# Attention results kept undivided, their softmax sums inverted apart and applied to turned results in the gating stage

## What is computed

```python
def _attention(src, Wq, bq, Wk, bk, Wv, bv, Wo, bo):
    q = (src @ Wq + bq).reshape(B, T, NHEAD, HEAD_DIM)   # k and v alike
    scores = jnp.einsum('bqhd,bkhd->bhqk', q, k) * scale
    probs = jax.nn.softmax(scores, axis=-1)
    out = jnp.einsum('bhqk,bkhd->bqhd', probs, v).reshape(B, T, d)
    return out @ Wo + bo
...
attn_out = _attention(src, Wq, bq, Wk, bk, Wv, bv, Wo, bo)
x = _ln(src + attn_out, ln1_g, ln1_b)
ff = _moe(x, gW, gb, W1, b1, W2, b2)      # softmax gates over 8 experts, two taken
return _ln(x + ff, ln2_g, ln2_b)
```

## Time and profile before

| | us |
|---|---|
| runs (3), median | 3671.24 (3670.13 to 3675.24) |
| the profiled execution | 3671.02 |
| its span, first to last instruction | 3669.3 |
| PE busy in the span | 3233.4 (88%) |
| DVE busy | 2949.0 (80%) |
| ScalarE busy | 2058.9 (56%) |
| POOL busy | 1198.9 (33%) |
| DVE's maxima L999, 2048 of them | 1285.6 |
| value products L1084 | 657.4 |
| first-pass products L1055 | 584.0 |

### The profile page before, as it was taken

How to read it: one execution, slowest core, us unless ns; L and a number is a source line. 1 busy time by engine, 2 the same in 40 slices (tenths; PEclk the granted TensorE clock), 3 DMA queues, 4 the chain that set the end, 5 groups by cost and what they waited for, 6 DMA issues and landing times. The chain is left out here.

```text
span 3669.3 us, 87949 instructions
## 1 busy us (share of the span) xinstructions
PE 3233.4 (88%) x34874; PEld 1861.1 (51%) x34875; DVE 2949.0 (80%) x4783; ACT 2058.9 (56%) x2972; POOL 1198.9 (33%) x974
## 2 busy tenths in 40 slices
PE   4889999999999999985999776996899999967776
PEld 1543333333333333344666542343787787756665
DVE  5778999999999999926666454775799999948986
ACT  0317777777777777763011265665675756434553
POOL 0310000000000000006011560000899999927875
PEclk8869999999999999996999877998999999989998
DMA  1552012020202020027222363333543434231110
GB/s 58 189 156 26 20 31 45 5 45 5 46 10 56 22 56 6 5 69 274 62 66 65 90 206 110 135 111 135 151 125 114 143 107 132 70 123 50 57 35 18
DMA packets 223122, 296.00 MB, mean 81 GB/s; under 512 B 72873, under 2 KB 159537, under 8 KB 220593
## 3 DMA queue, kind: packets, MB, share of 16 engines
q1 hardware_dynamic: 211616, 264.14, 25.3%
q0 software_dynamic: 6144, 17.05, 1.4%
q10 hardware_dynamic: 5008, 9.80, 0.7%
HBM read 174.35 MB, written 115.95 MB: 79 GB/s over the span
## 5 line engine op out<-in xcount | busy, mean ns | idle before, releaser
L999 DVE TENSOR_REDUCE att_maxima<-att_ps_m 128x1 f32<-128x512 f32 x2048 | 1285.6, 684 | 63.9 <-PE att_ps_m L1055 62.3
L954 ACT ACTIVATE att_probs<-att_ps_s 128x1024 f32<-128x1024 f32 x1024 | 999.4, 1022 | 280.3 <-PE att_ps_o L1084 267.8
L1084 PE MATMUL att_ps_o<-att_probs,held_vs 128*32 128x256 f32 x8192 | 657.4, 393 | 4.8 <-ACT att_probs L954 0.6
L2440 POOL TENSOR_TENSOR ss_ch<-ss_h,ss_c_rep 128x1024 f32<-128x1024 f32 x256 | 601.2, 2385 | 9.1 <-DVE ss_h L2527 9.1
L1055 PE MATMUL att_ps_m<-held_ks,held_qs 48*128 48x512 f32 x2048 | 584.0, 511 | 14.0 <-PEq L60 13.3
L2559 PE MATMUL ss_ps_u<-ss_diag,ss_dx_t 128*32 128x128 f32 x16384 | 475.3, 274 | 30.9 <-DMA ss_dx_t<-scratch_dx_t 15.0
L2559 PEld LDWEIGHTS ss_ps_u<-ss_diag,ss_dx_t 128*32 128x32 f32 x16384 | 455.5, 111 | 85.0 <-issue 68.7
L1055 PEld LDWEIGHTS att_ps_m<-held_ks,held_qs 48*128 48x128 f32 x2048 | 238.0, 188 | 456.8 <-DVE att_maxima L999 389.9
L1070 PE MATMUL att_ps_s<-held_qs,held_ks 50*128 50x512 f32 x2048 | 454.0, 405 | 2.8 <-ACT att_probs L954 0.8
L2479 ACT ACTIVATE ss_decay<-ss_delta,ss_a_neg 128x1024 f32<-128x1024 f32 x256 | 293.8, 1148 | 228.5 <-DVE ss_h L2527 206.8
L1084 PEld LDWEIGHTS att_ps_o<-att_probs,held_vs 128*32 128x32 f32 x8192 | 162.6, 108 | 361.6 <-issue 340.4
(11 more groups left out here) (394 smaller groups left out, 4485.2 us busy)
## 6 DMA issues: line engine op xcount, KB each, us to landing
ss_delta<-scratch_delta SPq DMA_DIRECT2D x256, 128.0 KB, 3.1
held_qs<-scratch_q SPq DMA_DIRECT2D x96, 128.0 KB, 4.6
held_ks<-scratch_k SPq DMA_DIRECT2D x96, 128.0 KB, 5.0
ex_x<-scratch_sorted_x SPq DMA_DIRECT2D x72, 132.0 KB, 2.1
scratch_sorted_y<-ex_y SPq DMA_DIRECT2D x72, 128.0 KB, 1.7
scratch_q<-held_parts SPq DMA_DIRECT2D x16, 512.0 KB, 4.7
scratch_k<-held_parts SPq DMA_DIRECT2D x16, 512.0 KB, 5.5
moe_w_w<-in_W SPq DMA_DIRECT2D x16, 512.0 KB
```

Source lines behind the costliest of these rows:

```text
L954: act.activation(probs[:, (2 * n + pair) % 4, :, :], ps_s[pair][:, :, :], ACT.Exp, scale=HD ** -0.5).then_inc(exp_done, 1)
L999: dve.tensor_reduce(maxima[:, j, at:at + 1], ps_m[plan.bank(key)][:, :], AX.X, ALU.max).then_inc(maxed, 1)
L1084: mm = pe.matmul(ps_o[h * VW:(h + 1) * VW, cols], vs[st // QC % 2][:, kt, h * VW:(h + 1) * VW], probs[:, (2 * n + h // 2) % 4, h % 2, cols ...
L2440: pool.tensor_tensor(ch[:, w.n % (CH_GROUPS * DQ), :], h[:, w.n % H_SLOTS, :], c_rep[:, w.ng, :], ALU.mult).then_inc(s["ch_ready"], 1)
```

## The change

The sums are no longer applied in attention. ScalarE's copy of `ps_o` has two slots now, and SP stores its rows of results as they are, by channel, to `scratch.outs`: four DMAs, one a head. Row 16 of each head, the sums of 512 queries, is spread by a DMA over 32 partitions of 16 columns, four DMAs a step. DVE inverts the 128x16 sums in key tile 10 (INVERT) and splits each inverse in a high part of the type fp32r and the rest; both go to `scratch.inv` by four DMAs. PE's transposes, ScalarE's second copy and POOL's division are gone, and the banks of `ps_m` are dealt out without `out`. All 16 columns after a head's values are ones.

In gating the results arrive turned, so `heads_t` is loaded directly, in two slots. The inverses of 16 heads in two parts (32 partitions) are spread over the 256 channels by two products with a pattern `own_head` of ones where a channel belongs to a head (`spread`), one step ahead of the rest, and DVE multiplies (`divide`, last in its step). PE's transposes of heads and ScalarE's copy are gone. POOL makes the pattern at the start, and SP copies it twice.

```diff
-                    pool.memset(by_head[:, :, HD:HD + 1], 1.0).then_inc(v_set, 1)
-                    pool.memset(by_head[:, :, HD + 1:VW], 0.0).then_inc(v_set, 1)
+                    pool.memset(by_head[:, :, HD:VW], 1.0).then_inc(v_set, 1)
...
-                if st > 0 and kt == 1:
-                    order.append(("out", st - 1))
...
+INVERT = 10
...
+                def store_outs(st):
+                    head, cols = places_of(st)
+                    sp.wait_ge(o_copied, st + 1)
+                    for h in range(QH):
+                        sp.dma_start(scratch.outs[(head + h) * HD:(head + h + 1) * HD, cols], o_sb[h * VW:h * VW + HD, st % 2, :]).then_inc(outs_stored[st % 2], 16)
+                    if st > 0:
+                        sp.wait_ge(sums_inverted, st)
+                    for h in range(QH):
+                        sp.dma_start(sums[h * VW:(h + 1) * VW, :], o_sb[h * VW + HD:h * VW + HD + 1, st % 2, :]).then_inc(sums_spread, 16)
+                def store_inv(st):
+                    head, cols = places_of(st)
+                    sp.wait_ge(inv_split, st + 1)
+                    for h in range(QH):
+                        sp.dma_start(scratch.inv[:, head + h, cols].rearrange("a (p j) -> p a j", p=VW),
+                                     inv_parts[h * VW:(h + 1) * VW, :, :].bitcast(F32)).then_inc(inv_stored, 16)
...
                 for st in range(1, STEPS):
+                    store_outs(st - 1)
                     if st % QC == 0 and st // QC + 1 < NQ:
...
-                    store_heads(st - 1)
                     if st + 1 < STEPS:
                         store_shift(st + 1)
+                    store_inv(st - 1)
...
-                        if st > 0 and kt == 4:
-                            divide(st - 1)
...
-                    act.activation(o_sb[:, :], ps_o[:, :], ACT.Copy).then_inc(o_copied, 1)
-                def copy_turned(st):
...
+                    if st >= 2:
+                        act.wait_ge(outs_stored[st % 2], st // 2 * QH * 16)
+                        act.wait_ge(sums_spread, (st - 1) * QH * 16)
+                    act.activation(o_sb[:, st % 2, :], ps_o[:, :], ACT.Copy).then_inc(o_copied, 1)
...
-                    dve.wait_ge(o_t_ready, st + 1)
+                    dve.wait_ge(sums_spread, (st + 1) * QH * 16)
                     if st > 0:
-                        dve.wait_ge(heads_ready, st)
-                    dve.reciprocal(sums[:, :], o_t[:, :, HD]).then_inc(sums_ready, 1)
+                        dve.wait_ge(inv_stored, st * QH * 16)
+                    dve.reciprocal(inv[:, :], sums[:, :]).then_inc(sums_inverted, 1)
+                    dve.wait_ge(sums_inverted, st + 1)
+                    split_high(dve, inv_parts[:, 0, :], inv[:, :]).then_inc(inv_high, 1)
+                    dve.wait_ge(inv_high, st + 1)
+                    split_low(dve, inv_parts[:, 1, :], inv[:, :], inv_parts[:, 0, :]).then_inc(inv_split, 1)
...
-                        if st > 0 and kt == 3:
+                        if st > 0 and kt == INVERT:
                             invert_sums(st - 1)
...
-                        if st > 0 and kt == 1:
-                            turn_out(st - 1)
...
                 load_heads(0, 0)
+                load_inv(0, 0)
+                load_inv(1, 1)
+                sp.wait_ge(own_set, 3)
+                for half in range(HALVES_QK):
+                    sp.dma_start(own_head[half * HEADS:(half + 1) * HEADS, :, :].bitcast(F32), own[:, :, :]).then_inc(own_copied, 16)
                 sp.dma_start(wo[:, :, :], io["Wo"].rearrange("(k p) c -> p k c", p=P)).then_inc(wo_loaded, 16)
...
+                def divide(g, slot):
+                    dve.wait_ge(heads_loaded[slot], (g // 2 + 1) * 16)
+                    dve.wait_ge(inv_spread, g + 1)
+                    dve.tensor_tensor(heads_t[:, slot, :, :], heads_t[:, slot, :, :], ps_h[:, :, :], ALU.mult).then_inc(heads_t_ready, 1)
...
-                run_stages(dve, GROUPS, (add_src, 1), (find_places, 4), (shift_logits, 3), (find_scale, 1), (take_best, 3), unroll=True)
+                run_stages(dve, GROUPS, (add_src, 1), (find_places, 4), (shift_logits, 3), (find_scale, 1), (take_best, 3), (divide, -1), unroll=True)
...
-                            mm = pe.transpose(ps_h[:, k, t * P:(t + 1) * P], heads[:, slot, t, k * P:(k + 1) * P], ident[:, :])
-                    mm.then_inc(heads_turned, 1)
+                    for k in range(KC):
+                        mm = pe.matmul(ps_h[:, k, :], own_head[:, k, :], inv[:, slot, :], start=True, stop=True)
+                    mm.then_inc(inv_spread, 1)
...
-                run_stages(pe, GROUPS, (turn_heads, 0), (count, 4), (turn_rows, 2), (product, 0), (logits, 2), unroll=True)
+                run_stages(pe, GROUPS, (spread, -1), (count, 4), (turn_rows, 2), (product, 0), (logits, 2), unroll=True)
```

94 lines of the change are left out of this document (43 added, 51 removed).

## The result

The changed kernel took 3681.14 us in the median of 20 executions (3669.94 to 3691.49), the kernel before 3672.53 us beside it (20 executions, 3664.55 to 3686.03): a ratio of 1.0021, 95% interval 1.0014 to 1.0029. The forecast was 3673.8 us with a range of 3664 to 3681 and a sum of +2.7 us on the kernel before; the ratio says +7.7 us (+5.1 to +10.7), just over the bound of 0.2%. So the change costs some 5 us more than forecast, and the result leans to "slower" where "no change" was thought likeliest.

The account below looks back on a forecast made before the run. PE and DVE, with no slack to speak of, bound attention; POOL's scatters bound gating. Attention -4.9, hand-over +6.1 and gating +1.5 make +2.7 on 3671.0 (0.2 under the median): 3673.8 us, range 3664 to 3681.

Parts of the forecast that it names:

- (a): Attention step: four transposes of the result leave PE, which both PE and DVE lose; -0.59 us a step.
- (b): Attention step: the old inversion in the fourth key tile, 0.24 us on DVE, goes; counted as -0.05 us a step.
- Rival C: Attention: DVE alone sets the pace, removed transposes give nothing, new operations add; +20 us, 3691 us, chance 0.04.
- (d): Eleventh key tile: three dependent DVE operations ahead of m_neg delay PE too; +0.49 us a step, bounds 0.22 and 0.74.
- Rival A: Attention: DVE's new operations find cover near m_neg, so the whole 0.64 a step stays; -12, 3659 us, chance 0.11.
- Hand-over: From attention's last copy to the next stage: exposed DMA issues and landings and DVE's operations add +6.1 us, low +3.7, high +9.1.
- Rival B: Hand-over: small DMA pieces land late, two round trips of 4.6 us each; total +8, 3679 us, chance 0.18.
- Gating: Stage after attention: later start and later first scatter, then POOL still sets the pace; +1.5 us, bounds +0.9 and +3.5.
- (f): Gating's start: pattern, its copies, spread and division delay the output product little; +0.3 us, bounds -0.3 and +2.1.
- (g): Gating's groups: DVE's added multiplication delays the first scatter by 1.25 us; 10.2 us a group stays under POOL's 10.34.
- (c): Attention: ScalarE's copy and POOL's division go, giving nothing except -0.4 us once in the last step.
- (e): Attention: SP's one store a step becomes twelve DMAs; costs nothing, unless scores wait for the shift in 7 steps.

Follow-up runs that it names:

- run 2: The changed kernel without DVE's inversion and its two parts in all steps but the first and last: ratio 0.9983 to the kernel before, step 41.24 us.
- run 4: The kernel before with one of the four transposes of a step's result: ratio 1.0003 to the kernel before, step 41.88 us.
- run 12: The kernel before with one transpose of four and, from the second step, ScalarE's copy of 128 columns instead of 512: ratio 0.9986, step 41.89 us.
- run 7: The kernel before with the three dependent DVE operations added ahead of m_neg on a tile of their own: ratio 1.0060, step 42.35 us.
- run 3: The changed kernel with the three inversion operations right behind m_neg instead of ahead of it: ratio 1.0041 to the kernel before, step 41.81 us.
- run 8: The changed kernel with the three inversion operations still together, in the seventh key tile instead of the eleventh: ratio 1.0007 to the kernel before, step 41.78 us.
- run 5: The changed kernel with the three inversion operations in three key tiles (sixth, eighth, tenth): ratio 0.9975 to the kernel before, step 41.27 us.
- run 1: The changed kernel again with no edit; its profile is the second trace: ratio 1.0024 to the kernel before, step 41.68 us.
- run 6: The changed kernel with sums' DMAs ahead of results' stores, gating's first spread in its own bank pair, three slots for inverses: ratio 1.0033 to the kernel before.
- run 9: The changed kernel with the three operations in three key tiles, repeated in another set: ratio 0.9977 to the kernel before, step 41.29 us.
- run 10: The changed kernel with the three operations in three key tiles, sums' DMAs ahead of results' stores, gating's first spread in its own bank pair: ratio 0.9956.

## Why the prediction was right or wrong

**The 30 steps, right in size: -5.9 without the fall, forecast -4.5.** (a) and (b) together gave 0.64 us as forecast (run 2). The reason given for (a) was wrong: "four transposes on PE ... both lose it" counts work, but three quarters of that work away changed nothing (runs 4 and 12). The sentence that the result's place among the three banks costs "nothing beyond (a)" had the two the wrong way round: by what runs 4 and 12 leave over, the place was all of (a). The sum held because the change removes both. Rival C, in the form in which it was put (PE's transposes don't count), was right on the transposes and wrong on the result.

(d) measured 0.44 for 0.49 in the changed kernel and 0.47 in run 7. The claim behind it, that whatever is put on VectorE "is paid in full", was too strong. It holds for 0.58 us in one piece, in any of three places (0.44 to 0.57 us: runs 2, 3, 8); in three pieces it costs 0.03 (run 5). Rival A's "find cover" came true for operations that stand apart and for no piece of 0.58 us; the 0.23 us of wait at m_neg covered 0.14 of it at most. By the Trainium skill (VectorE: DVE Perf Modes, The DRAIN you can't avoid) attention would have come to -7.5 us against the forecast's -4.9; without the fall it came to -6.7, between the two. No run has the old inversion alone, so its 0.24, on which the difference rests, stays unmeasured.

**What the prediction left out: the granted clock.** It took the clock in attention as given, 1.00 in every row it read the earlier trace rows. With the three operations in one piece at m_neg PE pauses 0.31 us once a step, and in none to two steps of a traced execution the clock falls to 1.2 GHz for 14 to 20 us, at 5.8 to 8.4 us each. In the five traces of kernels with a pause of 0.3 us or more in each step there are five falls (two in one, none in another), each 2.4 to 2.6 us after the end of such a pause; of the nine traces without one there is none, though PE is no less busy there: it is for 99.3 to 99.5% and VectorE for 93.5 to 95.2% of attention (the kernel before, runs 5 and 8) against 98.8 and 95.0% in run 1. Three operations in the kernel before bring it in (run 7), the same operations elsewhere keep it out (runs 5 and 8). Why it is this step and not the others, with the same pause, stays open, and that the pause is the cause and not something that goes with it would need PE's pause filled with other work, which wasn't tried. As a term of the sum it was some +6 us an execution, an estimate. One fall costs 5.8 us; the three traces with the changed kernel's attention (first, runs 1 and 6) have two, which makes 4. What the ratios leave once the steps are taken off is 2 us (run 2 against 1), 5 (runs 5 and 9 against the changed kernel), 8 (run 7) and 8 (run 8), each uncertain by 6 to 8 us. By it the clock is the largest of the terms that the forecast lacked.

**Hand-over: +4.7 for +6.1**, near the low bound. Landings were well judged (1.7 and 1.5 us for 1.9); issues were 0.43 us each for stores of results and of inverses (1.70 and 1.73 for four), forecast 0.5 and 0.65, and 0.60 for the sums, forecast 0.65. Rival B didn't come: small pieces landed in 1.5 to 1.7 us. The rule named there on writes under 512 bytes (the Trainium skill, DMA: Bandwidth & Descriptors, Specifications) shows in no landing here: runs of 64 bytes landed in 1.5 us, no later than the results' runs of 2048 bytes with 1.7.

**Gating: +5.6 and +4.4 for +1.5**, outside its bounds of +0.9 and +3.5. The step that failed is (f), +3.15 us at the first y addition in the first trace, +2.4 in the second, for +0.3 with bounds -0.3 and +2.1. The prediction let the output product start when the first division ended. PE's order has the second group's spread ahead of it, which waits for the division to free ps_h: one link left out, 1.3 us (with it out, in run 10, the product starts 1.5 us earlier, and the y addition 0.6 to 0.7 at the same rise of the clock). And the first spread came at 5.76 us, not 4.5. The third part is the clock again: PE has nothing to do for 16.80 us instead of 8.88, and the clock rises 15.6 us after the stage's start instead of 11.5, so that the product took 6.66 us for 5.92. How late it rises differs between traces (12.2 to 15.6 us after the start), and with it this part. (g) gave 1.14 us to the first scatter in the first trace (2.0 in the second), forecast 1.25. "POOL without gaps" was wrong, and y additions 10.2 us apart too: in the first trace they are 7.1, 7.1, 9.2, 10.6, 10.1, 12.6 and 9.0 us apart. The 12.6 has the wait in it: the last group's inverses are loaded behind the experts' weights, which adds a gap of POOL of 2.2 us in the first trace and 1.4 in the second. A load on a queue shared with 512 KB transfers was not costed at all.

**(c) and (e)**: the last step gained 0.8 us for 0.4; in none of the traces of the changed kernel did scores wait for the shift.

**The two signs.** Three terms came out better than forecast: the steps by 1.4 us, the last step by 0.4 and the hand-over by 1.4. Two came out worse: gating by 3 to 4 and the clock by about 6. In all, 5.9 + 0.8 = 6.7 gained, and 4.7 + 4.4 to 5.6 + some 6 lost: +8.4 to +9.6 stands against the +7.7 measured (+5.1 to +10.7), with no term for the start of attention. So it is luck in part that the time fell into the range: a term was missing and another was outside its bounds, and 3.2 us of errors the other way made up for some of it.

**The band.** "The bounds, with no more than two terms at an end" don't give 3666 to 3678.5: (d) at its upper bound alone is 30 x 0.25 = 7.5 us more, 3681, and attention and hand-over at their low bounds are 3663. Gating's upper bound is 2.1 + 1.25 = 3.35, not 3.5. With its own bounds the forecast's band would have reached over the range of 8 in 10.

## What to carry to other kernels

Where two engines run at nearly equal pace through a few shared banks, small operations were absorbed here when they stood apart (0.03 us of cost) and paid for the most part when they stood in one piece (0.44 to 0.57 us of 0.58): put the links of a chain one per iteration. Count what an edit does to the order in which banks are handed round before counting the work in them. And look for pauses of TensorE that an edit puts into a long busy stretch: here one of a third of a microsecond went with falls of the granted clock at six microseconds each.

## What the runs showed of the hardware

TensorE's granted clock fell in the middle of a stretch in which PE was busy for 98.8% of the time (1266.4 of 1282 us in run 1, the same schedule), 2.4 to 2.6 us after the end of a pause of 0.31 or 0.43 us; at the low level the pair of first-pass products took 2.16 us a half instead of 1.26 and the step 5.8 us longer. Why one pause is followed by a fall and the next isn't stays open. Stores of 32 KB to HBM, of 4 KB in runs of 64 bytes to HBM, and copies of 2 KB from one partition to 32 all landed 1.5 to 1.7 us after their issue (medians of the first trace). The second m_neg comes at 302.0 to 313.1 us over the twelve traces of the experiments, and at 313.1 and 309.2 us in the two traces of one kernel (runs 5 and 9).
